# A graph layer on one core: the one-hots' turned copies built from a table in DRAM instead of turned by TensorE

## What is computed

```
edge_in = concat([h[row], h[col], dist])           # 53125 x 129
e = silu(edge_in @ eW1 + eb1)
e = silu(e @ eW2 + eb2)                            # 53125 x 128
agg = segment_sum(e, row)                          # 3125 x 128
out = silu(concat([h, agg]) @ nW1 + nb1) @ nW2 + nb2
x = layernorm(x + out)
```

## Time and profile before

| | |
|---|---|
| time, median of 3 runs | 823.21 us (817.52 to 830.45) |
| the profiled execution's own time | 825.66 us |
| its span in the trace | 823.8 us |
| busy: PE, PE's weight loads | 623.5 us (76%), 497.4 us (60%) |
| busy: DVE, POOL, ACT | 477.3 us (58%), 446.0 us (54%), 320.4 us (39%) |
| mean granted clock of TensorE | 0.874 of full |
| DMA engines in the groups' stretch | some 15% busy, some 41 GB/s |

### The profile page before, as it was taken

The page is one execution under the profiler, slowest core; times in us unless marked ns, Lnnn a source line. Parts: engine busy times, 40 slices in busy tenths (PEclk is TensorE's granted clock), DMA queues, the critical chain, the costliest instruction groups (busy, mean ns, idle before and its releaser), DMA issues.

```text
span 823.8 us, 15564 instructions
## 1 busy us (share of the span) xinstructions
PE 623.5 (76%) x4815; PEld 497.4 (60%) x4815; DVE 477.3 (58%) x1582; ACT 320.4 (39%) x707; POOL 446.0 (54%) x459
## 2 busy tenths in 40 slices
PE   6874758769779878887787668868886759677796
PEld 3452546647667667665566556656665657566685
DVE  6883768978467746676567656856642223121155
ACT  6422232334334333433333333433434435343364
POOL 1056353447666665664676456655665656656500
PEclk9876958869889996999699879978997978899798
DMA  4111011111111111111111111111111111144201
GB/s 118 53 29 49 23 39 30 31 28 40 46 42 43 39 46 39 43 43 30 42 47 46 30 39 46 43 39 40 43 46 42 43 36 43 45 43 46 45 2 40
DMA packets 17077, 34.15 MB, mean 41 GB/s; under 512 B 8118, under 2 KB 9335, under 8 KB 17000
## 3 DMA queue, kind: packets, MB, share of 16 engines
q0 software_dynamic: 14080, 28.86, 14.4%
q1 hardware_dynamic: 2478, 3.36, 1.5%
q10 hardware_dynamic: 442, 0.93, 0.4%
HBM read 30.67 MB, written 2.40 MB: 40 GB/s over the span
## 4 chain that ended last, share of the span: by engine, by line
PE 57%; issue 14%; DVE 13%; another core or an unknown queue 11%; ACT 4%; DMA 1%; DVEq 0%; ACTq 0%
PE e_ps L625 19%; PE pre_ps L625 14%; PE seg_ps L625 12%; PE sort_ps L625 9%; PE turn_ps L729 3%; DVE load_hot L1060 2%; ACT e L515 1%; ACT hot L495 1%; DVE count L925 1%; DVE slot L965 1%; DVE row_hot L1056 1%; ACT h L509 1%; DMA x_sb<-in_x_dram 1%; DVE col_hot L1055 1%
## 5 line engine op out<-in xcount | busy, mean ns | idle before, releaser
L617 POOL DMA_INDIRECT q_rows<-q_table,q_index x440 | 442.4, 1006 | 333.5 <-issue 107.7
L1121 DVE TENSOR_TENSOR agg<-agg,seg_ps 128x125 f32 x416 | 93.6, 282 | 279.5 <-PE seg_ps L625 162.8
L625 PE MATMUL seg_ps<-hot,e 128*128 128x125 f32 x880 | 136.3, 302 | 58.3 <-ACT e L515 29.0
L625 PE MATMUL pre_ps<-ident_f,q_rows 128*128 128x128 f32 x440 | 134.8, 306 | 38.9 <-issue 38.9
L625 PEld LDWEIGHTS seg_ps<-hot,e 128*128 128x128 f32 x880 | 118.2, 209 | 67.1 <-issue 33.5
L515 ACT ACTIVATE e<-e_ps 128x512 f32<-128x512 f32 x110 | 65.7, 597 | 219.6 <-PE e_ps L625 116.2
L625 PE MATMUL pre_ps<-hotT,p_table 128*128 128x128 bf16 x1320 | 150.6, 237 | 0.0
L625 PE MATMUL e_ps<-w_sb,h 128*128 128x128 f32 x880 | 142.2, 310 | 0.0
L625 PEld LDWEIGHTS e_ps<-w_sb,h 128*128 128x128 f32 x880 | 119.6, 211 | 27.8 <-issue 27.8
L625 PEld LDWEIGHTS pre_ps<-hotT,p_table 128*128 x1320 | 126.0, 109 | 10.5 <-issue 0.6
L509 ACT ACTIVATE h<-pre_ps,eb_sb 128x512 f32<-128x512 f32 x110 | 75.5, 687 | 133.5 <-remote 74.5
(11 more groups left out here) (184 smaller groups left out, 505.6 us busy)
## 6 DMA issues: line engine op xcount, KB each, us to landing
q_rows<-q_table,q_index POOLq DMA_INDIRECT x440
q_table<-q_in_sb SPq DMA_DIRECT2D x1, 784.0 KB
x_sb<-in_x_dram ACTq DMA_DIRECT2D x1, 700.0 KB
q_table<-q_in_sb SPq DMA_DIRECT2D x1, 616.0 KB
out_dram<-x_sb SPq DMA_DIRECT2D x1, 364.0 KB
out_dram<-x_sb SPq DMA_DIRECT2D x1, 224.0 KB
w_in<-in_edge_weight_dram SPq DMA_DIRECT2D x1, 185.9 KB
dst_i<-in_dst_dram SPq DMA_DIRECT2D x1, 185.9 KB
```

Source lines behind the costliest of these rows:

```text
L617: P.indirect_dma_start(q_rows[:, g % RING, j, :], None, q_table, bass.IndirectOffsetOnAxis(ap=q_index[:, GT * g + j:GT * g + j + 1], axis= ...
L625: return nc.tensor.matmul(o, lhsT, rhs, start=start, stop=stop, **kw)
L1121: D.tensor_tensor(o, o, seg_ps[:, j * LO:(j + 1) * LO], ALU.add).then_inc(agg_added, 1)
```

## The change

For each chunk, nodes and weights are turned once, while they are still packed (one column a tile, 128 slots on the partitions), and not tile by tile after they have become one-hots.

- ACT (`split_weights`) writes `lo` and the three parts of the weight as four planes of `lay` (128 slots by up to 100 tiles, bf16). PE turns the four planes in a new part `LAY`, one step behind `READ`; ACT copies them to `layT` (`turn_lay`): tiles on the partitions, slots along them.
- SP stores `layT` to a table in DRAM, `slot_table` (plane, tile, slot), and waits for the landing. For every group it then issues two loads: plane 0's 512 slots, one row of 1 KB, read by all 128 partitions (`lo_wide`), and the three weight planes' 512 slots straight onto partitions 125 to 127 of `hotT`. It runs 4 groups ahead (`AHEAD`) and waits for `pre_ready` of group g - 4.
- DVE makes the turned one-hots itself: `one_hots_turned(g)` compares `lo_wide` with each partition's own number + 1 and writes `hotT[0:125]`. It stands two steps ahead of the group, first in DVE's step, in front of the sums.
- PE's `turn`, ACT's `place_weights` and `turned` are gone, and `w_parts` with them. `one_hots` makes 126 columns instead of 128 and no longer waits for PE's turn. `CARRY` is a part of its own on PE, with its own copy on ACT (`turn_rest`).

```diff
-def turned(g): ...  hotT <- hotT_ps        -def place_weights(g): ...  hot[:, LO:128] <- w_parts
+            def store_slots(k):
+                n = FULL[k]
+                sp.wait_ge(layT_ready, k + 1)
...
+                sp.dma_start(by_tile[where], layT[0:n]).then_inc(lay_stored[k % 2], 16)
+                sp.wait_ge(lay_stored[k % 2], 16 * (k // 2 + 1))
...
+            for g in range(GROUPS):
+                if g == 0 or chunk_of(g) != chunk_of(g - 1):
+                    store_slots(chunk_of(g))
+                if g >= AHEAD:
+                    sp.wait_ge(pre_ready, g - AHEAD + 1)
+                    sp.wait_ge(hotT_ready, g - AHEAD + 1)
+                slots = slot_table[:, GT * g:GT * g + GT, :].rearrange("v t s -> v (t s)")
+                sp.dma_start(lo_wide[:, g % AHEAD, :], slots[0:1].to_broadcast([128, GT * SLOT])).then_inc(slots_in[g % AHEAD], 16)
+                sp.dma_start(hotT[LO:128, g % AHEAD, :], slots[1:1 + SPLITS]).then_inc(slots_in[g % AHEAD], 16)
...
+            def turn_lay(k):
+                act.wait_ge(layT_ps_ready, k + 1)
+                if k:
+                    act.wait_ge(lay_stored[(k - 1) % 2], 16 * ((k - 1) // 2 + 1))
+                A.activation(layT[0:laid(k)], layT_ps[0:laid(k)], ACT.Copy).then_inc(layT_ready, 1)
...
             for m in range(GROUPS):
                 if m >= 1:
                     silu2(m - 1)
...
-                if m + 1 < GROUPS:
-                    place_weights(m + 1)
                 silu1(m)
-                if m + 1 < GROUPS:
-                    turned(m + 1)
-                    convert(m + 1)
+                convert(m)
...
+                elif name == LAY:
+                    pe.wait_ge(w_parted, k + 1)
+                    if k:
+                        pe.wait_ge(restT_ready, k)
+                    for v in range(1 + SPLITS):
+                        last = nc.tensor.transpose(layT_ps[0:laid(k), v, :], lay[:, v, 0:laid(k)], ident_b[:])
+                    last.then_inc(layT_ps_ready, 1)
...
                 first_layer(m)
                 if m >= 1:
                     segment(m - 1)
-                if m + 1 < GROUPS:
-                    turn(m + 1)
...
+            def one_hots_turned(g):
+                dve.wait_ge(slots_in[g % AHEAD], 32 * (g // AHEAD + 1))
+                D.tensor_scalar(hotT[0:LO, g % AHEAD, :], lo_wide[0:LO, g % AHEAD, :], next_p[0:LO, 0:1], None,
+                                ALU.is_equal).then_inc(hotT_ready, 1)
...
             for m in range(GROUPS):
+                if m + 2 < GROUPS:
+                    one_hots_turned(m + 2)
                 if m >= 2:
                     add_segments(m - 2)
```

More of the change, by code:

```diff
@@ L54 @@
 RING = 6
+AHEAD = 4
 ENC = 8192
@@ L139, in plan @@
         at(VECTOR, 85 + 2 * i, (RESIDUAL, 0, i))
+    for s in list(VECTOR):
+        for name, k, i in VECTOR[s]:
+            if name == READ:
+                at(TENSOR, s + 1, (LAY, k, 0))
 plan()
-assert all((READ, k, 0) in sum((VECTOR.get(s, []) for s in range(SURE[k - 1] // GT - 1)), []) for k in range(1, CHUNKS))
+assert all((READ, k, 0) in sum((VECTOR.get(s, []) for s in range(SURE[k - 1] // GT - 3)), []) for k in range(1, CHUNKS))
 CODED = {0: (0, COL0[1]), 1: (COL0[1], COL0[2]), 2: (COL0[2], COL0[3]), 3: (COL0[3], COL0[4]), 4: (COL0[4], ECOL)}
 CODED_STEP = {3: 2, 8: 3, 10: 4}
-CARRY_AT = {s: k for s, parts in TENSOR.items() for name, k, i in parts if name == CARRY}
 BAT0 = [sum(len(batches(j)) for j in range(k)) for k in range(CHUNKS)]
@@ L327, in build @@
         rows_in = [sem(f"rows_in{i}") for i in range(RING)]
+        lay_stored = [sem(f"lay_stored{i}") for i in range(2)]
+        slots_in = [sem(f"slots_in{i}") for i in range(AHEAD)]
         HOTS = 1 + V
@@ L416, in split_weights, with turn_rest @@
             def split_weights(k):
-                n, c = FULL[k], COLS[k]
+                n, c = FULL[k], laid(k)
                 bank = sort_ps[k % 2]
                 act.wait_ge(sort_read, k + 1)
-                where = [(starts(k) if k else 0, n, slice(0, n))]
-                if k == CHUNKS - 1:
-                    where.append((FLUSH, WIN, slice(n, c)))
-                parts = [bank[:, 0, :], w_rest[:, 1, :], w_rest[:, 2, :]]
-                for s in range(SPLITS):
-                    if s == 1:
-                        act.wait_ge(w_split, k + 1)
-                    for t0, size, cols in where:
-                        if cols.start:
-                            last.then_inc(w_full, 1)
-                            act.wait_ge(w_full, s + 1)
-                        last = A.activation(table(w_parts, t0, size, SPLITS)[:, :, s], parts[s][:, cols], ACT.Copy)
-                    if s == 0 and k < CHUNKS - 1:
-                        A.activation(rest[:], bank[:, :, n:n + WIN], ACT.Copy).then_inc(rest_ready, 1)
-                last.then_inc(w_parted, 1)
-            def starts(k):
-                return nc.values_load_multi_w_load_instructions(
-                    queue_i[0:1, k:k + 1], engines=(ENG.Activation,), min_val=0, max_val=EP * COL0[k] // SLOT,
-                    skip_runtime_bounds_check_because="no more full tiles than edges / 128")[1][0]
+                if k:
+                    act.wait_ge(layT_ps_ready, k)
+                A.activation(lay[:, 1, 0:c], bank[:, 0, 0:c], ACT.Copy)
+                if k < CHUNKS - 1:
+                    A.activation(rest[:], bank[:, :, n:n + WIN], ACT.Copy).then_inc(rest_ready, 1)
+                act.wait_ge(w_split, k + 1)
+                A.activation(lay[:, 0, 0:c], lo_i[:, 0:c], ACT.Copy)
+                A.activation(lay[:, 2:4, 0:c], w_rest[:, 1:3, 0:c], ACT.Copy).then_inc(w_parted, 1)
+            def turn_lay(k):
[3 more added lines that the diff above has]
+                A.activation(layT[0:laid(k)], layT_ps[0:laid(k)], ACT.Copy).then_inc(layT_ready, 1)
+            def turn_rest(k):
+                act.wait_ge(restT_ps_ready, k)
+                A.activation(restT[:], restT_ps, ACT.Copy).then_inc(restT_ready, 1)
             for n, (q0, q1) in enumerate(PAIR_SPANS):
@@ L481, in _ @@
                     split_weights(0)
+                    turn_lay(0)
                 if i == 9:
@@ L550, in deviation @@
                              scale=1.0 / NF).then_inc(ln_sd, 1)
-            place_weights(0)
-            turned(0)
-            convert(0)
             for m in range(GROUPS):
@@ L560, in _ @@
                         split_weights(k)
-                if m + 1 < GROUPS:
-                    place_weights(m + 1)
                 silu1(m)
-                if m + 1 < GROUPS:
-                    turned(m + 1)
-                    convert(m + 1)
+                convert(m)
+                for name, k, i in TENSOR.get(m, ()):
+                    if name == CARRY:
+                        turn_rest(k)
+                    elif name == LAY:
+                        turn_lay(k)
                 if m in CODED_STEP:
@@ L817, in node_out @@
                 last.then_inc(y_ready, 1)
-            p_parts(3)
+            p_parts(2)
+            part(LAY, 0, 0)
+            p_parts(1)
             part(OFFSET, 1, 0)
@@ L829, in _ @@
             pe.wait_ge(w2_in, 32)
-            turn(0)
             for m in range(GROUPS):
```

82 lines of the change are left out of this document (42 added, 40 removed).

## The result

The changed kernel takes 834.41 us (median of 4 runs, 832.31 to 837.81); the kernel before, on the same chip, 824.40 (4 runs, 817.52 to 830.45). Ratio 1.0138, 95% interval 1.0092 to 1.0185: some 10 us slower, where 3 us faster was forecast. Ratios and intervals in this document are of each kernel's fast runs, those within 1.5% of its quickest, and medians of all its runs, and on the occasion of a_behind to b_no_turn, where the kernel before spread from 813.6 to 837.8 us, the two differ by 0.5 to 1.2% (medians of all runs would give a_behind 0.998, a_read 1.004, b_read 0.992 and b_no_turn 0.991).

What follows compares the result with a forecast made beforehand. The prediction took POOL's gathers and pause, with PE's updates held meanwhile, to bound most groups. Terms -6 - 13 - 3 + 1 + 4 + 10 + 4 = -3 us gave 820 us against the 823.21 median; range 787 to 846.

Steps and rivals of the forecast that it cites:

- the store at a chunk's start: Chunks 1, 5, 6: chain from ACT's copy through store, load, compare to sums delays PE; 10 us lost, bounds 0 to 29.
- the removal: PE's turn gone, 6 us gained (bounds 0, 25); first layer no longer waiting for ACT's copy, 13 gained (8 to 33).
- the start: Kernel start: LAY adds a PE update, group 0's turn and copy go; 3 us gained, bounds 6 either way.
- The small costs: PE's turns of planes 1 us, DVE's compares in the first 14 groups 4, POOL's gathers beside the compare 4, all lost.
- The bottleneck: Most groups are timed by POOL's gathers and pause, 6.0 us a group; PE's updates stay unseen until POOL pauses.
- rival A: Held updates thin out with one PE update fewer a group, more idle counts: 42 us faster, 781 us; chance 0.28.
- rival B: PE gets out of step and POOL's runs join in 28 sortless groups: 34 us lost, 854 us; chance 0.15.
- What is queued behind the wait: Behind DVE's wait for SP's loads stand the sums of m - 2, then PE's segment m - 1; no separate size.
- DVE's compare: 110 compares on DVE at 0.3 us each, in front of the sums; 4 us lost in the first 14 groups (0 to 6).
- POOL beside it: POOL's gathers that meet DVE's new compare lengthen: 4 us lost, bounds 0 and 22.
- SP's traffic: SP's 220 loads move 14.4 MB more while the DMA engines are 15 to 37% busy: nothing lost.
- Rival C: New waits at their upper bounds, boundaries 29: 868 us if all come, 846 more credible; needs slow load landings; chance 0.11.

Runs made afterwards that it cites:

- a_behind: Changed kernel with DVE's one_hots_turned, and its wait for SP's load, behind the sums: 823.37 us, 1.0041 of the kernel before (updates held).
- b_no_turn: Kernel before without PE's turn, place_weights and ACT's turned copies, nothing in their place: 817.58 us beside 825.28, ratio 0.9957 (updates held).
- a_read: Changed kernel with READ of chunks 4 to 8 a step earlier: 828.27 us, 1.0155 of the kernel before (updates held).
- b_read: Control: kernel before with READ of chunks 4 to 8 a step earlier: 818.72 us, ratio 0.9976 (updates held).
- a_no_store_2: Changed kernel with only chunk 0's store, later groups loading chunk 0's slots: 835.61 us beside 839.64 for the kernel before, ratio 0.9943 (updates held).
- after_3: Changed kernel unaltered, measured again on another occasion: 858.00 us beside 839.64 for the kernel before, ratio 1.0208 (updates held).
- b_no_pool_4: Kernel before with SP's plain loads in place of POOL's gathers, on a held occasion: 631.56 us beside 839.64, ratio 0.7518.
- b_compare: Kernel before with one more, unused DVE compare a group: 679.28 us beside 678.58, ratio 1.0014 (updates not held).
- b_loads: Kernel before with two more SP loads a group that nobody reads: 678.85 us beside 678.58, ratio 1.0009 (updates not held).
- b_half: Kernel before with two gathers a group instead of four from group 6 on: 633.90 us beside 678.58 (updates not held).
- b_no_pool: Kernel before with SP's plain loads in place of POOL's gathers: 630.05 us beside 678.58 (updates not held).

## Why the prediction was wrong

Two terms of the sum failed, the store at a chunk's start (10 forecast, 22 measured) and the removal (-22 with the start, about -4 measured). Either alone turns the forecast's sign: with 22 for 10 the sum is +9, with -4 for -22 it is +15. The small costs, 1 + 4 + 4 in the sum, came out near nothing: a_no_store_2 pays them all and still gains as much as b_no_turn. So the runs add up to -4 + 22 = +18, which is what after_3 measured on the occasion of the 22; on the first occasion, with shorter holds at chunks 5 and 6, it was +10.

- **The bottleneck** was read rightly. POOL's gathers hold PE's updates (b_no_pool_4), the 6.0 us period stayed with the turn gone, and rival A (781) and rival B (joined runs in the sortless stretch; groups 76 to 104 took 171.2 us, 176.0 before) did not come. One thing in it was too strong: that nobody sees a held update until POOL has paused. Of the kernel before's 98 late starts of h and e, 36 fell while POOL was still in a run of gathers.
- **The store at a chunk's start is the first step that failed**, "3.3 to 9.7 us a time ... I take 10". It measured 22 us under the held condition, for the stores of all eight later chunks, most of it at chunks 5 and 6, and 5 under the free one (1.0058 against 0.9985 of 677, two occasions). The sum took `LAY`'s copy as coming at once after the transposes. But the transposes end in an update of PE, and the part on what bounds the kernel says that such updates are held: 8.1 us from the transposes' end to the copy here, 15.2 in after_3, and in neither end of my bounds. (Chunk 1's copy came at once, and its start lost less.) The chain as I had priced it, from the copy to the end of the sums, took 7.5 us (403.29 to 410.83), inside the 5.8 to 12.2 given. The other half of the miss is the clause "or nothing where PE's updates are held anyway": I took the hold for a cover, and it lengthens the chain.
- **What is queued behind the wait** was named (the sums, PE's segment) and not priced. a_behind prices it, with the reserve above: 1.0041 where the changed kernel has 1.0138.
- **The removal is the second step that failed.** It was sized at -6 - 13 and a -3 at the start, 22 us; its ceiling is -4 with the start included (b_no_turn, interval -10 to +3 on 825). The wait before the first layer went as forecast, and h's wait took its place (134.4 us from "remote" in b_no_turn, 74.5 before): "I take 40% of 33" should have been the lower bound of a quarter or less, since the next late thing was itself held.
- **The start** did not gain, 3.7 us lost where 3 gained were forecast, inside its bounds of 6 either way: group 0 begins at 82.2 us, 78.5 before. ACT's table copies came later, and not because of `LAY`'s own update, which was seen at once; beyond that the runs don't say why (a_no_store_2 has it too, b_no_turn starts group 0 at 73.0). The last two copies and the first layer behind them, in the changed kernel:

```profile
77.68 0.60 ACT L504 ACTIVATE p_table<-pre_ps 125x512 bf16<-125x512 f32 x1 [7.87 <-remote]
81.22 0.28 ACT L504 ACTIVATE p_table<-e_ps 125x128 bf16<-125x128 f32 x1 [2.95 <-remote]
82.22 0.45 PE L651 MATMUL pre_ps<-ident_f,q_rows 128*128 128x128 f32 x1 [18.76 <-ACT p_table L504]
```

- **DVE's compare** took 361 ns for 300 assumed; b_compare puts all 110 at 1 us, 3 at the upper end of its interval (free). **POOL beside it**: mean 1015 ns for 1006, which is the +4 forecast, but not from the compare: the 26 gathers of the changed kernel that ran beside this compare and no other DVE instruction took 950 ns on average, those beside none 943. (A longer gather meets more of DVE's instructions, so this choice leans to the short ones; but of all 440 gathers 35 took over 1.2 us, and 46 in the kernel before.) The Trainium skill's rule ("SBUF — State Buffer", Who interferes with whom) that a one-input compare may lock GpSimd out for its length is not what these gathers show.
- **SP's traffic** at nothing was right (b_loads). Store to load, 1.9 and 2.0 us, is near the 2 us that the Trainium skill gives as the fixed cost of one of GpSimd's DMAs ("DMA: Bandwidth & Descriptors", Anatomy of one DMA). From the first load's issue to the compare it took 3.0 to 3.4 us, more than the 2.3 estimated from it, and 2.6 to 3.0 from the second load's, for which the compare waits too.
- **Rival C** had the direction; its boundary term of 29 is nearer to the 22 measured than the 10 was. But it rests on slow landings, and the landings were quick (1.9 and 3.0 us): by its mechanism it was wrong, and the nearness is luck.

## What to carry to other kernels

When one engine's updates are seen late, price every new hand-over from that engine at the delay that the trace shows. Count those that the change adds where everything waits for them, and don't count those that it removes where a later one waits anyway. A wait put at the head of a step costs what stands behind it: place it last, or ask for the data a chunk earlier. And before sizing a removal, ask what is late next, and whether that is late for the same reason.

## What the runs showed of the hardware

- While POOL issues indirect DMAs (0.94 us each, 0.30 apart), PE's semaphore updates can be seen late: ACT, idle, started up to 8.1 us after the matmul's recorded end in the kernel before and up to 12.4 us in a_no_store_2. The first layer's update mostly comes about 1.05 us after POOL's run of gathers ends (46 of its 55 late ones behind a run); the second layer's more often comes within a run (27 of 43), as did the two at 396.88 and 403.29 above. PE's waits for ACT's h showed nothing of the kind: the second layer's matmuls started within 0.06 us in all 110 groups. With SP's plain loads in place of the gathers no update was late.
- The hold comes and goes from one occasion to another: at 107 of the 330 places ACT starts over 0.3 us late at 824 us, at none at 679, and the unchanged kernel before takes the one time or the other. What switches it is open. It is worth 150 us of this kernel, fifteen times the change that was studied.
- Free of it, the same kernel's bound is POOL's issue rate: 4 gathers in 5.0 us a group, where PE alone could do with some 45 us less in the whole (b_half, b_no_pool).
